# Blank rows written behind the last token of each expert instead of everywhere, token weights prepared under the image attention, and a new order around the token block's feed-forward layer

## The reference

```
h = group_norm(x);  q, k, v = wq h, wk h, wv h
x = x + wp softmax(q^T k / sqrt(c)) v                  # layer 0
x = x + o(attention(hyp(q), hyp(k), hyp(v)))           # layer 1
x = x + down(silu(gate h2) * (up h2))
x = x + sum over 2 experts of weight * expert(token)   # layer 2
```

## Time and profile before

| | us |
|---|---|
| median of three runs | 1533.67 |
| the profiled execution | 1548.29 |
| its span in the trace | 1546.5 |
| head, norm, first projections | 0 to 49 |
| image attention | 49 to 302 |
| token block: weights and first front | 302 to 382 |
| token block: four attentions and four lates | 382 to 947 |
| routing | 947 to 1093 |
| experts, 39 groups of 10.57 | 1093 to 1505 |
| write-out | 1505 to 1546.5 |

### The profile page before, as it was taken

How to read it: one execution, slowest core, us unless ns; L and a number is a source line. 1 busy time by engine, 2 the same in 40 slices (tenths; PEclk the granted TensorE clock), 3 DMA queues, 4 the chain that set the end, 5 groups by cost and what they waited for, 6 DMA issues and landing times. The chain is left out here.

```text
span 1546.5 us, 27783 instructions
## 1 busy us (share of the span) xinstructions
PE 1217.2 (79%) x9365; PEld 820.5 (53%) x9366; DVE 767.9 (50%) x1460; ACT 702.5 (45%) x1330; POOL 485.7 (31%) x411
## 2 busy tenths in 40 slices
PE   3989999452988698869777985440699999999992
PEld 1546666331334333433343343340588888888882
DVE  3755555156464657556655454542244444444441
ACT  3565454155567666756675652320232332333321
POOL 2021000101960294049305910557032332332331
PEclk9999999776999899979998996555899999999996
DMA  4576989824630662085108305994433433433326
GB/s 136 136 205 183 251 246 234 239 86 77 169 110 8 112 181 82 14 147 168 55 14 168 119 35 149 246 258 136 67 47 53 54 44 51 54 45 51 54 34 224
DMA packets 350675, 183.50 MB, mean 119 GB/s; under 512 B 271104, under 2 KB 337920, under 8 KB 350464
## 3 DMA queue, kind: packets, MB, share of 16 engines
q1 hardware_dynamic: 317056, 124.66, 35.3%
q0 software_dynamic: 25184, 56.64, 15.0%
q10 hardware_dynamic: 8352, 1.08, 0.5%
HBM read 38.66 MB, written 83.11 MB: 79 GB/s over the span
## 5 line engine op out<-in xcount | busy, mean ns | idle before, releaser
L2074 ACT ACTIVATE moe_hid<-moe_hbank,moe_b1T 128x256 f32<-128x256 f32 x312 | 130.2, 471 | 265.5 <-PE moe_hbank L2031 265.5
L2031 PE MATMUL moe_hbank<-moe_xT,l_w1T 128*128 128x256 f16 x1872 | 212.7, 274 | 45.7 <-DMA moe_xT<-rows_scratch 44.4
L2031 PEld LDWEIGHTS moe_hbank<-moe_xT,l_w1T 128*128 x1872 | 183.9, 98 | 68.2 <-issue 46.1
L2010 POOL DMA_INDIRECT acc_scratch<-moe_y,moe_meta x78 | 122.5, 1570 | 310.9 <-DVE moe_y L2101 288.2
L2046 PE MATMUL moe_ybank<-l_w2T,moe_hid_hi 128*128 x1248 | 206.4, 273 | 0.3 <-DVE moe_hid_lo L2088 0.3
L1111 ACT ACTIVATE block_probs<-block_bank 128x1024 f32<-128x1024 f32 (+1 forms) x192 | 144.8, 808 | 81.2 <-PE block_bank L870 67.2
L2046 PE MATMUL moe_ybank<-l_w2T,moe_hid_lo 128*128 x624 | 170.1, 273 | 0.0
L2086 DVE TENSOR_SCALAR moe_hid_hi<-moe_hid 128x2048 f16<-128x2048 f32 x39 | 47.8, 1227 | 203.4 <-ACT moe_hid L2074 203.4
L2046 PEld LDWEIGHTS moe_ybank<-l_w2T,moe_hid_hi 128*128 128x128 f16 x1248 | 122.1, 98 | 14.7 <-issue 0.6
L867 PE MATMUL block_bank<-block_qkT 128*128 128x512 f16 (+3 forms) x384 | 95.6, 338 | 39.6 <-DMA block_qkT<-block_stack 28.3
L732 POOL COPY block_stack<-block_stack 128x512 f16<-128x512 f16 x16 | 11.2, 700 | 315.1 <-ACT block_stack L1095 315.1
(11 more groups left out here) (354 smaller groups left out, 2550.2 us busy)
## 6 DMA issues: line engine op xcount, KB each, us to landing
rows_scratch<-l_blank SPq DMA_DIRECT2D x32, 1056.0 KB, 5.3
block_raw<-in_L_ffn_w POOLq DMA_DIRECT2D x32, 512.0 KB, 4.6
w_parts<-block_raw_hi POOLq DMA_DIRECT2D x32, 256.0 KB, 4.4
w_parts<-block_raw_lo POOLq DMA_DIRECT2D x32, 256.0 KB, 4.8
l_xs<-in_x SPq DMA_DIRECT2D x8, 512.0 KB, 7.2
x_scratch<-conv_mixed SPq DMA_DIRECT2D x8, 512.0 KB
block_t<-x_scratch SPq DMA_DIRECT2D x16, 256.0 KB, 4.1
acc_scratch<-block_res SPq DMA_DIRECT2D x16, 256.0 KB, 2.2
```

Of the source, the lines that this page charges most:

```text
L2010: pool.indirect_dma_start(acc, bass.IndirectOffsetOnAxis(ap=meta[r][:, t, 0:1].bitcast(U32), axis=0), y[r % 2][:, t, :], None, compute_op= ...
L2031: last = pe.matmul(hbank[:, c, :], w1T[:, e, wp, k, c * P:(c + 1) * P], xT[q][:, xp * CC + k, :], start=n == 0, stop=n == 5)
L2074: act.activation(hid[q][:, c, :], hbank[:, c, :], ACT.Gelu, bias=b1T[:, e, c:c + 1], scale=1.0 / (GAIN * GAIN)).then_inc(S["gelu_done"], 1)
```

## The change

- `make_blank_rows` and the 34 fills go. In `route` POOL makes the blank tile; each expert's region of the table gets one block more; DVE works out, when the counts are known, where each expert's tokens end, and SP writes 256 blank rows there for each of the 8 experts, and one blank block at the end of the table. DVE's plan gets four small operations more.
- The pieces of expert weights become a class `WeightPieces` that both stages use. 24 of 32 pieces (EARLY) are done by POOL within `conv_attention`, behind the x bias of each image (up to piece 5, 7, 11 and 24), and 3, 3, 2 and 0 in the token block's attentions.
- The token block's weights are prepared in `conv_attention`, in 10 chunks at steps 12 to 27: SP loads 256 KB, ACT makes the high part, DVE the low part, and SP transposes both by DMA (2 or 4 transposes a part) into the space of x of images that are done. The 16 strips of `first_front` go.
- In the token block hT has two buffers; `h_turned(0, pr)` runs one pair ahead of the projections; the norms' weights are waited for later.
- Within `attention`, statistics of the next batch, roots and the second norm come some steps earlier, and `h2_turned(b, 0)`, `h_turned(nb, 0)` and `h2_turned(b, 1)` move into its steps 20 to 22.
- `late` is reordered on PE, ACT and DVE: all projections of the next batch come before `gate(b, 3)` and before the `down`s. The old order on PE was: h2_turned 0, h2_turned 1, gate 0, output 2, output 3, gate 1, h_turned 0, gate 2, qkv 0, qkv 1, h_turned 1, h2_turned 2, h2_turned 3, qkv 2, qkv 3, h_turned 2, gate 3, qkv 4, qkv 5, h_turned 3, down 0, qkv 6, qkv 7, down 1, gate 4 to gate 7, down 2, down 3.

```diff
+EARLY = 24
@@ conv_attention, SP
+                    if n - 1 in SPLIT_AT:
+                        turn_chunk(SPLIT_AT.index(n - 1))
+                    if n + 2 in SPLIT_AT:
+                        load_chunk(SPLIT_AT.index(n + 2))
-                    for dst, src in fills[n::STEPS]:
-                        sp.dma_start(dst, src).then_inc(filled, 16)
+        SPLIT_AT = (12, 13, 15, 16, 18, 19, 21, 22, 26, 27)
@@ conv_attention, ACT and DVE
+                    act.activation(nat_hi[c % 2][:, :], nat[c % 2][:, :], ACT.Copy, scale=W_GAIN).then_inc(nat_hi_done, 1)
+                    dve.scalar_tensor_tensor(nat_lo[c % 2][:, :], nat[c % 2][:, :], W_GAIN, nat_hi[c % 2][:, :],
+                                             ALU.mult, ALU.subtract).then_inc(nat_lo_done, 1)
@@ conv_attention, POOL
+                ends = (0, 5, 7, 11, EARLY)
+                pieces.load(pool, 0)
+                pieces.load(pool, 1)
                 for b in range(B):
                     for c in range(CC):
...
+                    pieces.run(pool, ends[b], ends[b + 1], EARLY)
+                pieces.stored(pool, EARLY)
@@ token_block, attention on PE
+                        if m == ROOT_STEP + 2:
+                            pe.wait_ge(S["attn_done"], b * NR + NR - 1)
+                            h2_turned(b, 0)
+                        if m == ROOT_STEP + 3 and nb is not None:
+                            h_turned(nb, 0)
+                        if m == ROOT_STEP + 4:
+                            pe.wait_ge(S["h2T_lo"], b * PAIRS + 1)
+                            h2_turned(b, 1)
@@ first_front on PE
-                    for n in range(QKV_STRIPS):
-                        weight_strip(n)
+                    h_turned(0, 0)
+                    h_turned(0, 1)
                     for pr in range(PAIRS):
...
                         qkv(0, 2 * pr)
                         qkv(0, 2 * pr + 1)
-                        for n in strips_with(pr):
-                            weight_strip(n)
...
+                        if pr + 2 < PAIRS:
+                            pe.wait_ge(S["hT_lo"], pr + 1)
+                            h_turned(0, pr + 2)
@@ late on PE
+                    gate(b, 0)
+                    pe.wait_ge(S["hT_lo"], nb * PAIRS + 1)
+                    h_turned(nb, 1)
+                    gate(b, 1)
+                    qkv(nb, 0)
                     output(b, 2)
+                    pe.wait_ge(S["hT_lo"], nb * PAIRS + 2)
                     output(b, 3)
...
                     qkv(nb, 1)
...
+                    h_turned(nb, 2)
                     qkv(nb, 2)
                     qkv(nb, 3)
...
+                    gate(b, 2)
...
                     h2_turned(b, 2)
...
+                    h_turned(nb, 3)
                     qkv(nb, 4)
...
+                    h2_turned(b, 3)
                     qkv(nb, 5)
...
                     qkv(nb, 6)
                     qkv(nb, 7)
+                    gate(b, 3)
+                    gate(b, 4)
+                    down(b, 0)
                     down(b, 1)
...
                     gate(b, 5)
                     gate(b, 6)
                     gate(b, 7)
...
+                    down(b, 2)
+                    down(b, 3)
@@ late on DVE, its end (the two adds stood before log_factor and tangent_length)
...
                     stack_low(nb, 0)
+                    add(b, 0)
                     ff_product(b, 5)
+                    add(b, 1)
@@ route on SP
+                sp.wait_ge(S["tail_known"], 1)
+                for e in range(E_N):
+                    at = sp.value_load(tail_at[0:1, e:e + 1], min_val=0, max_val=(BLOCKS - 2) * GS)
+                    sp.dma_start(rows[bass.ds(at, GS), :].rearrange("(t p) r -> p t r", p=P), blank[:, :, :].bitcast(U32)).then_inc(S["filled"], 16)
+                sp.wait_ge(S["filled"], 16 * (E_N + 1))
```

More of the change, by code:

```diff
@@ L356, in _ @@
                     sp.wait_ge(half, 16 * B)
-                sp.wait_ge(filled, 16 * len(fills))
+                for q in range(2):
+                    sp.wait_ge(nat_turned[q], TURNED_PER_SLOT)
             @block.tensor
@@ L683, in token_block, with h_bank @@
         S = {n: s.sem(n) for n in names}
[L684 to L685 removed]
         FRONT_DVE, FRONT_ACT, LATE_DVE = 19, 6, 4
[L689 to L694 removed]
         def o_bank(pr):
             return 6 + pr if pr < 2 else 2 + pr
+        def h_bank(b, pr):
+            return ((5, 4, 5, 4) if isinstance(b, int) and b == 0 else (5, 5, 4, 4))[pr]
         def h2_bank(pr):
[L700 removed]
+            return (4, 4, 5, 5)[pr]
         def attn_buf(r):
[L704 removed]
+            return mixed[:, r % 2, :]
         with nc.Block() as block:
@@ L953, in down @@
                     last.then_inc(S["down_full"], 1)
-                def weight_strip(n):
-                    unit, k = strips[n]
-                    pe.wait_ge(S[f"w{unit}_loaded"], 16)
-                    if n >= 4:
-                        pe.wait_ge(S["w_lo"], n - 3)
-                    for o in range(weights[unit].shape[0] // P):
-                        last = pe.transpose(bank[:, n % 4, o * P:(o + 1) * P], staged[unit][:, o, k * P:(k + 1) * P], ident[:, :])
-                    last.then_inc(S["w_full"], 1)
@@ L1432, in attention @@
                             second_norm(b, 0)
+                        if m == ROOT_STEP + 2 and nb is not None:
+                            normalised(nb, range(0, 4))
+                        if m == ROOT_STEP + 4:
+                            h2_low(b, 0)
+                        if m == ROOT_STEP + 5 and nb is not None:
+                            h_low(nb, 0)
                 def last_round(b):
```

439 lines of the change are left out of this document (208 added, 231 removed).

## The result

The changed kernel takes 1519.38 us (median of 4 executions, 1513.44 to 1521.70) against 1533.37 us before: a ratio of 0.990, 95% interval 0.9883 to 0.9917. It is 14 us faster, where 34.5 were forecast. The profiled execution of the changed kernel is the fastest of the four, with a span of 1511.7 us; that of before lay 14.6 us above its median. So the two spans, 34.8 us apart, must not be compared as they stand. The stages tell where the difference comes from. The columns are read from the timelines: the first row maximum to the last residual (image attention), from there to the first scores of the token block, the four attentions and lates together up to the routing's first operation, and the routing up to the first expert matmul. Before has two traces of the same program; the second has a span of 1530.6 us (experiment 1).

A forecast was written before the change was run, and what follows sets the result against it. PE bounds the attentions, hand-off order the stretches between, POOL's scatters the routing. Gains 2 + 0 + 15 + 15 + 2.5 = 34.5 us take 1533.7 to 1499, range 1474 to 1530.

The forecast's parts named there:

- pieces and chunks in the image attention: Image attention: holding DVE costs 6 us in steps 8 to 23, 3 each in images 0 and 3, cancelling the fills' 12.
- The sign of being wrong: Image attention: the forecast is wrong if the steps of images 1 and 2 grow over 8 us.
- the full hold: DVE in the image attention: each two-input operation waits out the POOL operation it meets, losing 0.83 us on average.
- The rival on SP: Steps 12 to 23: slower transposes overfill SP, PE waits 45 us; decides from 1.84 us each; 1544 us, chance 0.07.
- The first rival: Image attention: hold in full, DVE bounds steps 8 to 27, cost 27 us in place of 12; 1514 us, chance 0.13.
- Head: Kernel start: SP's first load no longer waits behind the barrier of the blank tile; gain 2 us.
- Fills: Image attention: removing fills from SP's queue gains 8.5 us in the last two steps and 3.5 in steps 4 to 7.
- First front: Start of token block: earlier statistics 7 us, two hT buffers and no strips 6, last strips 1.5; gain 15 (12 to 18).
- Lates: Batches 0 to 2: reordering and moved transposes take 83.6 us to 78 with attention's 1.7; gain 5 each, 15 in all.
- The last late: Late of the last batch: two groups of transposes with their waits are gone; gain 2.5 us.
- Routing: Routing: the new blank-row fills, some 12 us, are covered by POOL's scatters; 0 (−6 to +6).
- The span: Whole profiled run: 1546.5 us less the summed gain of 34.5 gives 1512.

The follow-up runs named there:

- experiment 1: The kernel before, unchanged, run and traced once more: 1534.52 us, ratio 0.9999.
- experiment 4: The kernel before with only the blank tiles and the changed kernel's routing in place of the blanket fills: 1523.49 us, ratio 0.9931.
- experiment 5: The changed kernel with POOL's full operations for 24 pieces in the image attention but without their loads and stores there: 1527.00 us.
- experiment 3: The changed kernel with POOL's piece operations in the image attention cut to 8 columns and memsets filling the time, loads and stores kept: 1511.23 us, ratio 0.987.
- experiment 2: The changed kernel with all 32 pieces of expert weights back in the token block, 8 in each attention: 1498.54 us, ratio 0.9785.
- experiment 11: The changed kernel without the 36 transposes of token weights on SP, so the token block computes with zero weights: 1505.46 us, ratio 0.9803.

## Why the prediction was wrong, point by point

**The size.** 14 us in place of 34.5, with the sign right and the time within the range. The term of the sum that failed is pieces and chunks in the image attention.

**Pieces and chunks: the step that failed.** The step took 6 us for steps 8 to 23, out of bounds of 0 and 26, and 3 and 3 beside it. These 12 us were all for the hold of DVE; of SP it said that its transposes "stand beside PE's work", and put them at nothing. Measured, pieces and chunks cost 26 to 27 us (259.1 and 258.0 us of image attention, against 232.0 without them in experiment 4), of which the chunks without the pieces are 1.3. With the fills' gain the whole part is a loss of 16 to 17 us, where 0 was forecast and 15 was its upper end. The sign of being wrong also came: images 1 and 2, steps 8 to 24, grew from 118.1 us to 127.4 and 132.9, more than 8.

It was not the hold that was priced too low: alone it costs 4.8 us (experiment 5), and without it the changed kernel loses 8.1 less (experiment 3), both under 12. What stood at nothing is the pieces' traffic on the transposes in SP's queue. It costs 17.7 us with DVE at its old speed (experiment 3 over 2), and SP's same 76 issues in steps 12 to 28 take 117 us in place of 96. Two readings led there. "Their traffic is 24 MB instead of 34" counted bytes. The fills stood in SP's own queue behind the step's transposes; the pieces' loads and stores are on another and meet every transpose, which then takes 1.7 to 1.9 us in place of 1.4. And SP's room was counted at 1.3 us a transpose.

The reading of L1518 was wrong too, although it did not make the miss: I took its median, but the mean is what sums up. The mean was in the trace of before (lines of DVE, 380 to 950 us, shapes apart), 0.30 us above the least where the median is 0.13 above it:

```profile
L1518 DVE SCALAR_TENSOR_TENSOR block_turned_lo<-block_h,block_turned_hi 128x512 f16<-128x512 f32 x12 | 11.9, 989 | 17.4 <-ACT block_turned_hi L1158 17.4
```

In the changed kernel the low part of the probabilities lost 0.38 us on average and the chunks' 0.40, in its second trace 0.27 and 0.08, all well under the full hold of 0.83. The rule of the Trainium skill in "SBUF — State Buffer", section "SBUF: two separate sides", is borne out in kind by the runs: an operation with two SBUF inputs is held by POOL operations that read (1606 ns), not by memsets (1225 ns). That the loser waits for the whole of the other's operation each time they meet, no run here shows.

The rival on SP named the right mechanism, at 0.07. Its own sum does not fit: it counts transposes alone, and at the measured 1.72 and 1.84 us in steps 12 to 24 it would give nothing, since its point was 1.84. The backlog measured is about 12 us (experiment 11), much of it in steps 24 to 28, which it left out. The first rival's 27 us are near the measured cost by luck, since the hold has only 5 to 8 of them.

**Head.** SP's first load and PE's first work came 2.0 us earlier, as forecast. Of these 1.4 reach the first row maximum against the second trace of before, but over the twelve traces with this head it lies anywhere between 49.2 and 54.1 us, so that this gain is not told from scatter.

**Fills.** 3.5 in steps 4 to 7 was 3.4 in the first eight steps; 8.5 at the end was 6.7, since a wait of 0.9 stays.

**First front.** 15 forecast, 13.7 measured, by the mechanism given.

**Lates.** The forecast of 76.3 us counts a late from the last weighted sum. So counted they took 72.0, 74.2 and 73.5 us, with the waits at their places, and 72.0, 78.4 and 72.0 in the second trace. An attention, counted likewise, grew by 2.3, 4.4, 3.4 and 0.4 us, not by 1.7. The term of 15 us was too small, as 7.6 us a batch went, 6.6 in the second trace: the attention with late was also freed of five of eight pieces. With these back (experiment 2) it is 4.7 a batch against my 5, and this is partly luck: the lates gained 9.5 where 7.3 were forecast, and the attentions lost 4.8 where 1.7 were. Besides the three groups of transposes, ACT's two table loads of 1.28 us, formerly among its last exponentials, now stand ahead of exponentials that PE waits for (1.66 us at 579.02 in the second attention):

```profile
575.02 1.28 ACT L1161 ACT_TABLE_LOAD   x1
...
576.64 1.28 ACT L1136 ACT_TABLE_LOAD   x1
...
579.02 0.39 PE L895 MATMUL block_bank<-block_qkT 128*128 128x512 f16 x1 [1.66 <-ACT block_probs L1136]
```

The last late did not gain 2.5 but lost 1.2; with its two groups put back it takes 59.7, so the moved transposes help it and its other edits cost it more. Which of them was not tried.

**Routing.** 0 forecast, 0 measured against the second trace. The scatters end 119 us after its start, as forecast.

**The span.** 1512 was forecast and 1511.7 measured, and that is chance: 13 us of it were the wait in the first trace, which I had not set apart although the execution lay 14.6 us above the median.

## What to carry to other kernels

Background work is priced by what it shares, not by its bytes or by the busy share of its engine: here POOL was free in the image attention, yet its pieces held DVE and, what cost more, stretched the transposes of a queue that hand-offs depend on, and they cost about 1 us each there against 0.45 us in an attention of the token block, where DVE and SP have room. Add up the issue time of the queue that everything waits for, at the duration its operations have beside the new traffic, and compare it with the stretch; two rivals that load the same stretch should be added before one of them is called unlikely. And when a profiled execution lies off the median, take a second trace before building a sum on its waits.

## What the runs showed of the hardware

- A transpose by DMA that SP issues in 1.24 to 1.31 us took 1.7 to 1.9 on average, and up to 4.94, beside loads and stores of 512 and 256 KB on POOL's queue, and 1.45 when these stood in SP's queue; without them it took 1.40.
- POOL memsets of 0.95 us, back to back, hold DVE's two-input operations little or not at all: 1225 ns against 1224 for the low part of the probabilities, 732 against 682 for that of the chunks.
- Beside POOL operations that read, the same two averaged 1357 to 1641 and 764 to 1300 ns, with large differences between executions of one program (1606 and 1493, 1077 and 764).
- The routing of the kernel before took 145 us in one execution and 132 in another, that of the changed kernel 132 and 146. Of the four long ones among fourteen traces three are all that were traced on one of the chips.
